# A fifth unit of each batch is multiplied by C on GpSimd, and the order of some steps at the start and at the end is changed

## The reference, cut to what matters

```
xz = xn @ in_proj_w.T;  x_in, z = split(xz)
u  = silu(conv(x_in));  dt_r, B, C = split(u @ x_proj_w.T)
dt = softplus(dt_r @ dt_proj_w.T + b);  A = -exp(A_log)
h  = h * exp(dt * A) + (dt * u) * B      # for each of 256 steps, 512 channels, 16 states
y  = sum over the 16 states of h * C;  y = (y + u * D) * silu(z)
```

## Time and profile before

| | |
|---|---|
| median of the runs | 584.17 us (583.55 to 586.76) |
| the profiled execution: time, span | 582.02 us, 580.2 us |
| VectorE busy | 514.3 us, 89% |
| GpSimd busy | 454.9 us, 78% |
| TensorE busy | 430.7 us, 74% |
| ScalarE busy | 405.0 us, 70% |
| granted TensorE clock, mean | 0.909 of full speed |

### The profile page before, as it was taken

One profiled execution on the slowest core, in us unless ns is written; L12 is line 12 of the kernel. 1 busy time (PEld: TensorE's weight loads), 2 busy tenths in 40 slices (PEclk: granted clock), 3 DMA queues, 4 the chain that ended last, 5 costly groups with the idle time before them and its releaser, 6 DMA issues. The chain is left out here.

```text
span 580.2 us, 7357 instructions
## 1 busy us (share of the span) xinstructions
PE 430.7 (74%) x2444; PEld 350.1 (60%) x2444; DVE 514.3 (89%) x567; ACT 405.0 (70%) x887; POOL 454.9 (78%) x319
## 2 busy tenths in 40 slices
PE   8976665677687678669687767779776766676876
PEld 7646445546575567458585656568665655565655
DVE  2368799999999999999999999999999999999523
ACT  3682678758866989398857988598956976675134
POOL 4059959999997989978997899978997899992011
PEclk9975977999899898999788989989899979887989
DMA  8293013201430134002420154014410133000001
GB/s 255 72 330 114 0 67 118 108 1 50 161 110 1 28 148 163 2 28 72 149 92 1 31 181 128 0 29 147 125 39 11 32 155 125 1 18 2 0 1 36
DMA packets 22365, 45.37 MB, mean 78 GB/s; under 512 B 3684, under 2 KB 13556, under 8 KB 22328
## 3 DMA queue, kind: packets, MB, share of 16 engines
q1 hardware_dynamic: 22328, 44.92, 23.8%
HBM read 42.52 MB, written 2.39 MB: 77 GB/s over the span
## 5 line engine op out<-in xcount | busy, mean ns | idle before, releaser
L518 POOL TENSOR_TENSOR hs<-dtu,Br 128x1024 f32<-128x1024 f32 x127 | 296.9, 2361 | 9.2 <-DMA Br<-bc_rows 9.2
L678 ACT ACTIVATE ring<-dt,Aneg 128x256 f32<-128x256 f32 x512 | 213.1, 465 | 79.7 <-DVE hs L889 75.7
L882 DVE TENSOR_TENSOR_SCAN ring<-ring,hs 128x1024 f32<-128x1024 f32 x96 | 219.0, 2281 | 6.4 <-ACT ring L678 6.2
L1229 PE MATMUL sums<-ident,hs 128*128 128x128 f32 x1024 | 147.4, 298 | 65.6 <-DVE hs L889 61.0
L1229 PEld LDWEIGHTS sums<-ident,hs 128*128 128x128 f32 x1024 | 129.1, 154 | 81.4 <-DVE hs L889 73.8
L889 DVE TENSOR_TENSOR hs<-ring,Cr 128x1024 f32<-128x1024 f32 x96 | 117.6, 1225 | 3.3
L527 POOL TENSOR_TENSOR hs<-hs,Cr 128x1024 f32<-128x1024 f32 x32 | 75.5, 2358 | 47.1 <-DVE hs L882 47.1
L882 DVE TENSOR_TENSOR_SCAN hs<-ring,hs 128x1024 f32<-128x1024 f32 x32 | 72.7, 2270 | 0.0
L1297 PE MATMUL PY<-wqkvo,xT 128*128 128x256 f32 x168 | 48.1, 437 | 0.0
L602 ACT ACTIVATE conv<-PX,par 128x256 f32<-128x256 f32 x30 | 15.3, 560 | 46.9 <-PE PX L1177 46.7
L1297 PEld LDWEIGHTS PY<-wqkvo,xT 128*128 128x128 f32 x168 | 39.1, 233 | 7.6
(11 more groups left out here) (199 smaller groups left out, 644.5 us busy)
## 6 DMA issues: line engine op xcount, KB each, us to landing
Br<-bc_rows SPq DMA_DIRECT2D x32, 512.0 KB, 5.0
Cr<-bc_rows SPq DMA_DIRECT2D x32, 512.0 KB, 4.3
xg<-in_x SPq DMA_DIRECT2D x8, 256.0 KB, 2.8
out<-fin SPq DMA_DIRECT2D x7, 256.0 KB, 4.5
hs<-in_ada_wT SPq DMA_DIRECT2D x3, 512.0 KB, 5.0
win<-in_in_wT SPq DMA_DIRECT2D x2, 512.0 KB, 6.9
hs<-in_W_emb SPq DMA_DIRECT2D x2, 512.0 KB
gate<-gate_rows SPq DMA_DIRECT2D x8, 128.0 KB, 3.1
```

The source lines that it names most:

```text
L518: nc.gpsimd.tensor_tensor(hs[:, g % DBUF], dtu[:, b % 2, dc, :].unsqueeze(1).to_broadcast([P, NQ, T]), Br[:, NQ * q:NQ * q + NQ, :], ALU.m ...
L678: ins = nc.scalar.activation(ring[:, g % 2, j, :], dt[:, b % 2, dc, :], ACT.Exp, scale=Aneg[:, c:c + 1])
L882: V.tensor_tensor_scan(driven if by_pool(g) else decays, decays, driven, 0.0, ALU.mult, ALU.add).then_inc(s_scan_done, 1)
L1229: ins = M(YT[:, c, :], hs[:, g % DBUF, j, P * c:P * c + P], ident[:, :], is_transpose=True, start=False, stop=(q == UPC - 1 and j == NQ - ...
```

## The change

`by_pool` names unit 11 too, and no longer the very first unit 1 (g = 1), which DVE then multiplies itself. So GpSimd has 39 units in place of 32. Unit 11 is the last of its channel group, and a new function `deferred` keeps its sum out of those that are put off: PE adds it at g = 11, in order. BEHIND stays 5.

For batch 1, `due_later` becomes `due_by` with a delay for each step. The quarters of its input projection go to PX, PY, PX, PY; in_proj_1 is issued right after in_proj_0 (g = -2), ahead of `setup_emb`, in_proj_2 at g = 3, in_proj_3 at g = 5. ACT does conv_last_tap_0 at g = 2 and conv_last_tap_1 at g = 3. The gate rows go through PZ, and `setup_gate8` waits for both parts of `setup_emb`.

At the end, PE turns group 2 of batch 7 back at unit 12, ACT copies it at unit 14 (before: 13 and 15), each ahead of its other steps. `rstd2(6)` stands behind the two `last_rstd` of the first norm. The k product and the last output product of batch 7 go over the halves j of the contraction outside and wait for each half by itself.

```diff
 def by_pool(g):
-    return g % U in (1, 5, 9, 13)
+    return g % U in (1, 5, 9, 11, 13) and g > 1
+def deferred(g):
+    return by_pool(g) and g % UPC != UPC - 1
 def summed_after(g):
-    return g - 1 if g >= 1 and by_pool(g - 1) else None
+    return g - 1 if g >= 1 and deferred(g - 1) else None
 def sums_until(g):
-    return g + 2 if by_pool(g) else g if g >= 1 and by_pool(g - 1) else g + 1
+    return g + 2 if deferred(g) else g if g >= 1 and deferred(g - 1) else g + 1
-def due_later(g, slot):
-    if g == U + slot + 2:
+def due_by(g, slot, by):
+    if g == U + slot + by:
...
         def xz_bank(b, h):
-            return (PX, PY, PZ, ring[:, 0, 0:2, :])[h] if b == 0 else PX
+            if b == 0:
+                return (PX, PY, PZ, ring[:, 0, 0:2, :])[h]
+            return (PX, PY, PX, PY)[h] if b == 1 else PX
... GpSimd
-                    if b is not None and not (b == LAST_B and slot > 20):
+                    if b is not None and not (b == LAST_B and slot > 20) and not (b == LAST_B - 1 and step is rstd2):
...
             last_rstd(1, mv1, ve1, rs1, nb1, s_last_st1, s_last_rs1)
+            rstd2(LAST_B - 1)
... ScalarE
+                if g == LAST_B * U + 14:
+                    last_yg((2,), PX)
-                    b = (due_soon if step is normalize0 else due_later if step is conv_last_tap_1 else due)(g, slot)
+                    late = 1 if step in (conv_last_tap_0, conv_last_tap_1) else 0
+                    b = due_soon(g, slot) if step is normalize0 else due_by(g, slot, late)
-                if g == LAST_B * U + 15:
-                    last_yg((2,), PX)
... VectorE
-                dve.wait_ge(s_emb_mm, 1)
-                V.tensor_tensor(gate8[:, :], PY[0:NB, 0, :], gb8[:, :], ALU.add).then_inc(s_gate8_ready, 1)
+                dve.wait_ge(s_emb_mm, 2)
+                V.tensor_tensor(gate8[:, :], PZ[0:NB, 1, :], gb8[:, :], ALU.add).then_inc(s_gate8_ready, 1)
... TensorE
+                elif b == 1:
+                    if h >= 2:
+                        pe.wait_ge(s_tap_done, 3 * DC * b + 6 * (h - 1))
...
-                pe.wait_ge(s_xT_ready, KD * NB)
-                for h in range(KD):
-                    for j in range(KD):
+                for j in range(KD):
+                    pe.wait_ge(s_xT_ready, KD * LAST_B + j + 1)
+                    for h in range(KD):
...
-                if 0 <= g < NB * U and not by_pool(g):
+                if 0 <= g < NB * U and not deferred(g):
                     sum_states(g // U, g % U)
...
+                if g == LAST_B * U + 12:
+                    pe.wait_ge(s_last_yg, 2)
+                    last_back((2,), PX, 3)
...
-                    b = (due_later if step in (in_proj_1, in_proj_2, in_proj_3) else due)(g, slot)
+                    b = due_by(g, slot, -2 if step is in_proj_1 else 1 if step is in_proj_2 else 2 if step is in_proj_3 else 0)
```

More of the change, by code:

```diff
@@ L1092, in _ @@
                                    (34, stats2), (40, finish)):
-                    b = (due_later if step in (conv_taps_0, conv_taps_1) else due)(g, slot)
+                    b = due_by(g, slot, 2 if step in (conv_taps_0, conv_taps_1) else 0)
                     if b is not None:
@@ L1141, in setup_emb @@
                 for k in range(KC):
-                    ins = M(PY[0:NB, 0, :], cT[:, k, :], adaT[:, k, 2], start=(k == 0), stop=(k == KC - 1))
+                    ins = M(PZ[0:NB, 1, :], cT[:, k, :], adaT[:, k, 2], start=(k == 0), stop=(k == KC - 1))
                 ins.then_inc(s_emb_mm, 1)
@@ L1436, in last_steps @@
                 keep_on(6)
-                pe.wait_ge(s_hT_ready, KD * NB)
-                for c in range(TC):
-                    half_rows(last_half(c), 3, b, c).then_inc(s_o_mm, 1)
+                for j in range(KD):
+                    pe.wait_ge(s_hT_ready, KD * LAST_B + j + 1)
+                    for c in range(TC):
+                        ins = M(last_half(c), xnT[:, j, P * c:P * c + P], wqkvo[:, 3, j, :], start=False, stop=(j == KD - 1),
+                                skip_group_check=True)
+                        if j == KD - 1:
+                            ins.then_inc(s_o_mm, 1)
             def in_proj_0(b):
@@ L1475, in _ @@
                     last_back((0, 1), PX, 2)
-                if g == LAST_B * U + 13:
-                    pe.wait_ge(s_last_yg, 2)
-                    last_back((2,), PX, 3)
                 if g == LAST_B * U + 14:
```

## The result

The changed kernel is slower, as forecast: a median of 603.88 us (601.64 to 604.81, 4 runs) against 583.95 us (583.55 to 586.76, 4 runs) for the kernel before. The ratio is 1.0325, with a 95% interval of 1.0281 to 1.0369. The forecast was 599 with a range of 589 to 608. The profiled execution took 603.42 us, with a span of 601.6 us against 580.2 us before. So the trace has 21.4 us to explain, where the sum made from the rows said 15.25.

The account below looks back on a forecast made before the run. VectorE was taken to bound the batches, holding GpSimd. Batches +26.35, start -6.8, end -4.3 make +15.25 us on 582.02: 597.3, as a median 599.4, given as 599; own range 594 to 604, with rivals 589 to 608.

Parts of the forecast that it names:

- What bounds the kernel: In the eight batches VectorE never stops (89% of the span busy) and GpSimd (78%) is held by it.
- the stall: VectorE idles at `gate_y(2)` because GpSimd multiplies unit 11 behind inputs 16; 5.6, five times 3.8 and 2.15 us lost, batches 0-6.
- GpSimd's wait ahead of multiply 9: Each batch, GpSimd's idle time before multiplying unit 9, waiting for its scan, was to grow from 1.59 to some 3 us.
- the knock-on valued at 0: TensorE, ACT and DMAs behind `gate_y(2)` keep their place after it: 0 us, bounds 0 to 1.5 us a batch.
- Batch 7: Last batch: no wait at `gate_y(2)`, 1.14 us gained, but TensorE ends the batch; gain of 0.5 us, ends 0 and 1.5.
- The start: Before the batches: `gate_y(0)` 4.7 us earlier and the 2.06 us wait before scan 6 gone; 6.8 us gained, ends 4 and 8.
- The end: Batch 7's first norm no longer waits for `rstd2(6)` on GpSimd; 4.3 us gained in all, ends 3 and 5.
- with the warmer matmuls: At the end, TensorE goes on at once after its fill matmuls: 3.94 us gained, taken as 4.0.
- the output product by halves: Last output product: two of four half products run before the second half is there; 0.3 us gained (0 to 0.5).
- The offset: The profiled execution was 2.15 us under the median of the runs, so 597.3 us became 599.4 as a median.
- the third: Rival: TensorE's steps behind unit 11's sum come late for convolution or ACT, 1 us more in seven batches; median 606; 17 in 100.
- The rule of occupancy: Skill page's rule: improve the engine with the highest occupancy first; by it the forecast said the change is a gain.

## Why the prediction came out as it did

**What bounds the kernel, and the stall.** Right, and shown. VectorE waited where it was said, for what was said: 26.5 us in batches 0 to 6 against 26.85, batch by batch 5.58, 3.8 (3.62 in batch 5) and 2.13 against 5.6, 3.8 and 2.15. The chain behind it (multiply 9, inputs 15, `rstd0`, `softplus_0`, inputs 16, then the new multiply) took 15.81 us against 15.83. That GpSimd's order and not the multiply itself is the cause is shown by the kernel that only reorders it: 569.41 us with the same instructions.

**One step of this part was wrong without a cost.** GpSimd's wait ahead of multiply 9 was to grow from 1.59 to some 3 us. It was 1.83. The waits ahead of its multiplies did grow, from 47.1 to 53.2 us, but elsewhere in the batch. What mattered, that it waits there for the scan and so carries nothing over from one batch to the next, held.

**The step that failed: the knock-on valued at 0.** The prediction left TensorE, ACT and the DMAs at 0 behind the stall, with 0 to 1.5 us a batch as bounds, and gave a chance of 17 in 100 to 1 us a batch. The trace has 5.6 us between the stalls, 0.8 us a batch. The largest piece lies between `gate_y(3)` of batch 6 and `gate_y(0)` of batch 7, 17.43 us where it was 15.71. What the rows show of the cause is TensorE's clock. The two windows of 100 to 520 us, before and then after (length, busy us and matmuls of each engine, granted clock, DMA share, GB/s):

```profile
100.00:520.00 420.00, 314.24 (x1826) 259.20 (x1825) 413.36 (x420) 321.25 (x714) 380.19 (x254) 0.93 0.23 74
```

```profile
100.00:520.00 420.00, 318.08 (x1725) 263.94 (x1723) 381.51 (x389) 302.41 (x672) 367.30 (x241) 0.87 0.22 73
```

TensorE was busy longer for 101 matmuls fewer, at a granted clock of 0.87 in place of 0.93. The sum behind each idle stretch of 5.0 to 6.7 us ran at the lower level. The two stretches of the kernel with the multiply alone show what that level costs when it falls on the projection: 1.81 us. I had used this for the one sum that ends the wait, where 1.95 against a measured 1.97 was right, and not for later matmuls.

The largest piece is the one at the end of batch 6. Two blocks of 8 matmuls on TensorE for the attention, and VectorE behind them, in the changed kernel:

```profile
509.78 1.87 PE L1348 MATMUL PZ<-blockmask,qT 128*128 128x4 f32 x8 [1.13 <-ACT kT L738]
511.51 2.05 PE L1359 MATMUL PZ<-vm,kT 128*128 128x128 f32 x8
513.60 0.61 DVE L949 SCALAR_TENSOR_TENSOR att<-PZ,rk,blockmask 128x128 f32<-128x128 f32 x2 [2.30 <-PE PZ L1359]
```

The same two blocks in the kernel with 60 matmuls ahead of the sum:

```profile
508.93 1.06 PE L1348 MATMUL PZ<-blockmask,qT 128*128 128x4 f32 x8 [1.12 <-ACT kT L738]
509.84 1.14 PE L1359 MATMUL PZ<-vm,kT 128*128 128x128 f32 x8
```

There VectorE waits 0.57 us and the stretch takes 15.71 us, both as in the kernel before. So these 1.7 us are the clock. The waits at the convolution go with one block too, the 8 matmuls of `q_times_att` (the attention's product with q), some 7 us ahead of it. Behind `gate_y(3)` of batch 2, in the kernel before, the changed kernel, and the kernel with 60 matmuls:

```profile
233.34 1.16 PE L1355 MATMUL PY<-att,qT 128*128 128x128 f32 x8 [1.14 <-DVE att L940]
```

```profile
243.14 1.76 PE L1367 MATMUL PY<-att,qT 128*128 128x128 f32 x8 [0.70 <-DVE att L949]
```

```profile
240.07 2.08 PE L1367 MATMUL PY<-att,qT 128*128 128x128 f32 x8 [1.36 <-DVE att L949]
```

The fourteen traces of this case hold 70 such stretches (five each, from `gate_y(3)` of batches 1 to 5 to the next `gate_y(0)`). In 34 the block took 1.69 to 2.08 us, and VectorE waited at the convolution in each of them; in the other 36 it took 1.15 to 1.17, and VectorE waited in none. In the changed kernel all five are of the slow kind and their waits come to 2.5 us, against 0.4 in the one slow stretch of the kernel before. With the 1.7 us of batch 6 that is 3.8 of the 5.6 us; where the rest lies stays open. The kernel without unit 11's move lost 1.3 us over the same span (`gate_y(2)` of batch 0 came 4.68 us earlier than in the kernel before, `gate_y(3)` of batch 7 only 3.41), with three slow stretches of its own.

What sends the clock down at that block is not shown. The idle stretch ahead of the sum is not enough, and not needed: the kernel with the multiply alone has the whole stall and two slow stretches of five. The kernels without the stall have up to three. The kernel with 60 matmuls has next to no idle time there and five of five, with longer waits (5.7 us in all). So I can say that the lower level was the cost, and not that the stall alone caused it.

**Batch 7.** Forecast -0.5 us, found +0.2. As foreseen, the decays of unit 15 came late, by 0.67 us, and TensorE's sum ended the batch. The multiply less did help for a while: from scan 11 to scan 12 it was 3.97 us in place of 5.26. But ahead of scan 9 VectorE waited 1.02 us for the output product, where it had not waited before, and with the 0.67 us nothing was left of the gain.

**The start.** Forecast 6.8 us with ends of 4 and 8, found 4.9 in the trace and 5.9 in the medians of the kernel with the start alone. The chain was right: `gate_y(0)` started at 56.10, in the forecast 54 to 57, without a wait, and the 2.06 us ahead of the scan of unit 6 are gone. Two things that the sum did not have took back 3.3 us, so the chain itself gave some 8.2, more than the 6.8. TensorE's 32 first matmuls on the conditioning, before (first row) and after:

```profile
8.91 3.64 PE L1124 MATMUL PX<-cT,hs 128*128 128x8 f32 x32
```

```profile
9.38 4.97 PE L1133 MATMUL PX<-cT,hs 128*128 128x8 f32 x32
```

They ran slower in this execution, and VectorE's first `dt` came 1.7 us later (32.84 against 31.13). This is no part of the change, since in the kernel with unit 11 one unit earlier, whose start is the same, they took 3.71 us. The other is told below.

**The end.** The mechanism was right and its size was off: 6.0 us in the trace against 4.3. TensorE after its fill, with no idle time, in the changed kernel:

```profile
578.85 1.26 PE L1120 MATMUL sums<-ones 97*128 97x256 bf16 x10
579.94 0.38 PE L1385 MATMUL ring<-ident,xhat 128*128 128x128 f32 x2
...
581.53 1.99 PE L1416 MATMUL ring<-xnT,wqkvo 128*128 128x256 f32 x8
```

From the second moments (577.14) to the first turned half it is 2.80 us in place of 6.91, a gain of 4.1 and so the 4.0 of the prediction. From there to the k product it is 1.59 in place of 2.86: without the idle time the matmuls between ran at 2.4 GHz. I had said "with the warmer matmuls" and counted 0.06 us for them. The 0.3 us for the output product by halves cannot be told from nothing.

**The offset.** The sum was made on an execution 2.15 us under its median, and I added that to the result. The changed kernel's profiled execution was only 0.5 us under its own. In the trace the sum missed by 6.1 us (597.3 against 603.4), as a median by 4.5 us (599.4 against 603.9). Of the rivals, the third, the stall that spreads, had the right sign for the rest, and its 606 us lies nearer to the measured 603.9 than my 599. That the forecast came as close as it did is partly luck: the start gave 1.9 us less than forecast and the end 1.7 us more, which cancel.

**The rule of occupancy.** The forecast set the Trainium skill's Perfetto Trace Analysis, section Identifying the Most-Contended Engine, against the rows. VectorE was the engine with the highest occupancy, and taking eight multiplies from it cost 28 us when done alone. The same move with GpSimd's program in another order cost nothing. In this case the rule names the right engine, but says nothing on whether the engine that takes the work over has it in time.

## What to carry to other kernels

When work moves to an engine with idle time, look where in that engine's program it will stand, and where its idle time lies: the idle time counts only if it lies between the data being ready and the moment at which the result is wanted. Fix such a stall where the late result is made, by moving it ahead in its producer's order, together with the next one in that order; moving the consumer back or speeding up a link in the middle gave back little or nothing here. And when TensorE's lower clock level is likely, price it for each block of matmuls that another engine waits for, and not only for the first one behind the stall: here it was worth 3.8 us.

## What the runs showed of the hardware

**A small VectorE instruction beside GpSimd.** In the start of the changed kernel, VectorE's timeline has two instructions of one form behind each other:

```profile
73.17 1.82 DVE L1021 TENSOR_SCALAR m1s<-mods,par 128x8 f32<-128x8 f32 x1
74.90 0.22 DVE L1021 TENSOR_SCALAR m1b<-mods,par 128x8 f32<-128x8 f32 x1
```

The first took 1.82 us; in the kernel before the same one took 0.23. GpSimd meanwhile:

```profile
72.58 2.38 POOL L525 TENSOR_TENSOR hs<-dtu,Br 128x1024 f32<-128x1024 f32 x1
```

In ten of the fourteen traces GpSimd is at work on such a tile when this instruction starts. There it took 1.55 to 1.99 us (1.61 without the fifth multiply, 1.74 with units 11 and 13 one unit earlier, 1.74 with the start alone), and ended 0.02 to 0.03 us after GpSimd's did, each time. In the other four, one of them with the changed start (unit 3 in place of unit 11), GpSimd had nothing to do at that moment, and it took 0.23. So it waited there for GpSimd's instruction to end. VectorE's scans and multiplies take their 2.28 and 1.22 us beside the same work, and what sets this small instruction apart was not tested.

**TensorE in the first 15 us.** With the same instructions, the 32 matmuls above took 3.64 to 3.71 us in seven of the profiled executions and 4.58 to 4.99 in the other seven. Two kernels that differ by 1 to 2 us can owe it to this.

**What keeps the upper level costs too.** 32 bf16 matmuls took 3.66 us and 60 took 6.71, and TensorE issues in order: 60 of them held the sum back by 0.4 us and saved 0.93.
